# GpSimd adds the attention scores of four column tiles; TensorE sums the denominators from two such sums

## What is computed

```python
h = relu(layernorm(x))
Wh, We = h @ W, entity_embs @ W
scores = (Wh @ a1)[:, None] + (We @ a2)[None, :]
e = where(scores > 0, scores, 0.2 * scores)
e = where(adj > 0, e, -9e15)
attention = softmax(e, axis=1)
x = x + elu(attention @ entity_embs + h)
h = relu(layernorm(x))
x = x + (adj == 1) @ h + h
```

## Time and profile before

| | |
|---|---|
| time, median of three runs | 415.71 us (415.42 to 417.8) |
| the profiled execution's own time | 416.58 us |
| its span in the trace | 414.8 us |
| TensorE, VectorE, ScalarE, GpSimd busy | 87%, 74%, 44%, 27% of the span |
| mean granted clock of TensorE | 0.947 of full |

### The profile page before, as it was taken

The page is one execution under the profiler, slowest core; times in us unless marked ns, Lnnn a source line. Parts: engine busy times, 40 slices in busy tenths (PEclk is TensorE's granted clock), DMA queues, the critical chain, the costliest instruction groups (busy, mean ns, idle before and its releaser), DMA issues. The chain is left out here.

```text
span 414.8 us, 5569 instructions
## 1 busy us (share of the span) xinstructions
PE 360.7 (87%) x2295; PEld 126.6 (31%) x2295; DVE 306.9 (74%) x329; ACT 184.0 (44%) x205; POOL 112.1 (27%) x165
## 2 busy tenths in 40 slices
PE   0679935999976889999978999998899999999996
PEld 0254611221121113233222332332223323334564
DVE  3182068979997998989979789799897899934211
ACT  1130104566644656754356556544565546542100
POOL 5189801111111114125111241101112498000500
PEclk9967765999999699999999999999899999999999
DMA  6999997777869687669885997899999950000011
GB/s 226 236 214 201 212 213 145 132 126 134 147 113 156 90 128 127 120 110 134 151 120 98 141 162 132 89 108 104 88 92 92 107 59 0 2 2 0 2 52 51
DMA packets 15848, 47.85 MB, mean 115 GB/s; under 512 B 1552, under 2 KB 1616, under 8 KB 15568
## 3 DMA queue, kind: packets, MB, share of 16 engines
q0 software_dynamic: 14656, 44.05, 70.1%
q1 hardware_dynamic: 1168, 3.46, 2.2%
HBM read 111.46 MB, written 1.05 MB: 271 GB/s over the span
## 5 line engine op out<-in xcount | busy, mean ns | idle before, releaser
L589 ACT ACTIVATE yp<-yp,tbias 128x1024 f32<-128x1024 f32 x128 | 146.7, 1149 | 118.5 <-DVE yp L806 117.2
L806 DVE SCALAR_TENSOR_TENSOR yp<-s8b,t8neg,am 128x1024 f32<-128x1024 f32 x128 | 162.3, 1288 | 17.5 <-PE pb L1078 16.8
L1065 PE MATMUL pb<-yp,enta 128*64 128x512 f32 x512 | 140.6, 631 | 27.6 <-ACT yp L589 27.3
L722 DVE TENSOR_TENSOR am<-am,vx 128x2048 uint16<-128x2048 uint16 x64 | 79.2, 1237 | 1.8 <-ACT vx L517 1.8
L384 POOL DMA_DIRECT2D am<-adj_t x64 | 35.2, 558 | 163.3 <-DVE yp L806 163.0
L1078 PE MATMUL pb<-yp,onesf 128*32 128x512 f32 x512 | 69.1, 612 | 0.1
L1065 PEld LDWEIGHTS pb<-yp,enta 128*64 128x64 f32 x512 | 28.7, 139 | 103.0 <-ACT yp L589 69.6
L993 PE MATMUL pb<-am,h 128*64 128x512 bf16 (+1 forms) x432 | 55.8, 383 | 0.0
L993 PEld LDWEIGHTS pb<-am,h 128*64 128x64 bf16 x432 | 26.5, 111 | 40.5 <-issue 29.7
L393 POOL DMA_DIRECT2D am<-adj_t x14 | 10.0, 711 | 58.5 <-DVE yp L806 58.5
L1078 PEld LDWEIGHTS pb<-yp,onesf 128*32 128x32 f32 x512 | 10.2, 109 | 39.3 <-issue 36.7
(11 more groups left out here) (145 smaller groups left out, 259.5 us busy)
## 6 DMA issues: line engine op xcount, KB each, us to landing
am<-adj_t POOLq DMA_DIRECT2D x78, 512.0 KB, 7.7
edge<-adj_t POOLq DMA_DIRECT2D x6, 512.0 KB, 9.4
enta<-ent SPq DMA_DIRECT2D x1, 1040.0 KB, 5.2
xs<-xt SPq DMA_DIRECT2D x1, 1024.0 KB, 10.7
out<-yp SPq DMA_DIRECT2D x4, 256.0 KB, 2.0
mats<-eye SPq DMA_DIRECT2D x1, 256.0 KB, 6.2
wt_sb<-w_t SPq DMA_DIRECT2D x1, 32.0 KB, 2.1
a_sb<-a_cols SPq DMA_DIRECT2D x1, 0.5 KB, 2.0
```

Of the source, the lines that this page charges most:

```text
L589: sc.activation(y, y, ACT.Exp, bias=tbias[:, at:at + 1]).then_inc(exp_done, 1)
L722: v.tensor_tensor(at, at, vx[:, b % 2, 0:width(b)].bitcast(U16).unsqueeze(1).to_broadcast([P, tiles(b), width(b)]), ALU.bitwise_xor).then_ ...
L806: v.scalar_tensor_tensor(out=yp[:, n % YS, 0:W], in0=s8b[:, b % 2, 0:W], scalar=t8neg[:, at:at + 1], in1=am[:, (chunk0[b] + c) % RING, jt ...
L1065: t.matmul(acc2(b)[s * D:(s + 1) * D, :], enta[:, tile_at(b, jt), 0:D], yp[:, n % YS, s * HALF:(s + 1) * HALF], start=(jt == 0), stop=(jt ...
```

## The change

GpSimd gets an addition. For each group of four steps it adds their four score buffers into one of two new buffers `ysum` (128 x 1024 float32): nothing at the first step of the group, `yp + yp` at the second, `ysum + yp` at the third and fourth. That is done for the first 120 steps, 90 additions in all, each of which waits for `exp_done`, and the later ones for the sum before (`y_summed`). TensorE makes denominators only at steps that are multiples of 8, from the two sums, four matmuls in place of sixteen. The last eight steps keep the old way. `pv_done` rises with each step's numerators, and VectorE waits for `y_summed` (in the last steps `dens_done`) as well before it overwrites a score buffer. There are five score buffers in place of four, two `edge` buffers in place of four, and four edge loads in place of six go to them; the other 16 go into the ring. The step numbers of `FIN`, `LONE_AT` and the first `PIECE_AT` shift, and the four diagonal additions of `own` are spread over four steps.

```diff
-YS = 4
+YS = 5
+DIRECT_STEPS = 8
...
-PIECE_AT = (47, 51, 57, 61, 67, 71, 79, 83, 88, 92, 96, 100, 104, 108, 112, 116, 120, 124)
+PIECE_AT = (48, 52, 58, 62, 68, 72, 80, 84, 89, 93, 97, 101, 105, 108, 112, 116, 120, 124)
...
-EDGES = 4
-RINGED = 6
-LOAD_AT = (28, 34, 56, 62, 70, 74)
+EDGES = 2
+RINGED = 4
+LOAD_AT = (28, 34, 66, 70)
...
+    POOLED = STEPS_ALL - DIRECT_STEPS
+    def sums_with(n):
+        return n // 8 + 1 if n < POOLED else POOLED // 8 + (n - POOLED) // 2 + 1
...
+            def add_scores(n):
+                a = ysum[:, n // 4 % 2]
+                if n % 4 == 0:
+                    return
+                pool.wait_ge(exp_done, n + 1)
+                if n % 4 == 1:
+                    if n >= 8:
+                        pool.wait_ge(dens_done, n // 8)
+                    g.tensor_tensor(a, yp[:, (n - 1) % YS], yp[:, n % YS], ALU.add).then_inc(y_summed, 2)
+                else:
+                    pool.wait_ge(y_summed, n)
+                    g.tensor_tensor(a, a, yp[:, n % YS], ALU.add).then_inc(y_summed, 1)
...
+                if n < POOLED:
+                    add_scores(n)
...
                     dve.wait_ge(pv_done, n - YS + 1)
+                    if n - YS < POOLED:
+                        dve.wait_ge(y_summed, n - YS + 1)
+                    else:
+                        dve.wait_ge(dens_done, sums_with(n - YS))
...
-                if jt % 2 == 1:
-
-                    if jt == 1 and b >= 1:
-                        pe.wait_ge(den_sb, first[b])
-                    for r in range(2):
-                        for s in range(2):
-                            at = r * D + s * 32
-                            mm = t.matmul(dens[at:at + 32, :], onesf[:, 0:32],
-                                          yp[:, (n - 1 + r) % YS, s * HALF:(s + 1) * HALF],
-                                          start=(jt == 1), stop=(jt == NT - 1), tile_position=(0, at))
-                    mm.then_inc(pv_done, 2)
+                if n % 8 == 0 and 0 < n <= POOLED:
+
+                    b2 = (n - 1) // NT
+                    if n - 8 == b2 * NT and b2 >= 1:
+                        pe.wait_ge(den_sb, first[b2])
+                    pe.wait_ge(y_summed, n)
+                    denominators(ysum[:, 0], ysum[:, 1], n - 8 == b2 * NT, n == (b2 + 1) * NT)
+                if n >= POOLED and n % 2 == 1:
+                    denominators(yp[:, (n - 1) % YS], yp[:, n % YS], False, n == STEPS_ALL - 1)
```

More of the change, by code:

```diff
@@ L121, in graph_layers @@
     VROWS = [t + 1 for t in SHIFTS]
-    FIN = [dict(den=1, inv=2, bc=3, t=4, e=4, c=6, xc=7, sq=7, var=8, vs=9, h=11, hi=11, r=12, mid=12, lo=14)
+    FIN = [dict(den=2, inv=3, bc=4, t=5, e=5, c=7, xc=8, sq=8, var=9, vs=10, h=12, hi=12, r=13, mid=13, lo=15)
            ] * (NB - 1)
-    LONE_AT = 6
+    LONE_AT = 10
+    POOLED = STEPS_ALL - DIRECT_STEPS
+    def sums_with(n):
+        return n // 8 + 1 if n < POOLED else POOLED // 8 + (n - POOLED) // 2 + 1
     ctx = ExitStack()
@@ L143, in graph_layers @@
         yp = sb("yp", [P, YS, 2 * HALF], F32)
+        ysum = sb("ysum", [P, 2, 2 * HALF], F32)
         s8b = sb("s8b", [P, 2, 2 * HALF], F32)
@@ L305, in graph_layers @@
         pv_done = sem("pv_done")
+        y_summed = sem("y_summed")
+        dens_done = sem("dens_done")
         den_sb = sem("den_sb")
@@ L349, in own_at @@
         def own_at(v):
-            return PIECE_AT[v] - 3
+            return PIECE_AT[v] - 6
         block = ctx.enter_context(nc.Block())
@@ L458, in deviations, with own @@
                 g.tensor_tensor(rstd[:], rstd[:], mhalf[:], ALU.pow).then_inc(rstd_ready, 1)
-            def own(w):
+            def own(w, tiles_of):
                 p, j = ORDER[w]
@@ L465, in own @@
                 pool.wait_ge(edges_in[w], 16)
-                for i in range(SUB):
+                for i in tiles_of:
                     e = edges(w)[:, i, at + i * P:at + (i + 1) * P]
                     g.tensor_tensor(e, e, eyeb[:], ALU.add, saturate=False).then_inc(own_ready, 1)
+            def add_scores(n):
[10 more added lines that the diff above has]
+                    g.tensor_tensor(a, a, yp[:, n % YS], ALU.add).then_inc(y_summed, 1)
             def edges_at(u):
@@ L485, in _ @@
                 for w in OWN:
-                    if w < PIECES and n == own_at(w):
-                        own(w)
+                    if w < PIECES and 0 <= n - own_at(w) < SUB:
+                        own(w, (n - own_at(w),))
+                if n < POOLED:
+                    add_scores(n)
             for w in OWN[4:6]:
-                own(w)
+                own(w, range(SUB))
             deviations(NB - 1)
             for w in OWN[6:]:
-                own(w)
+                own(w, range(SUB))
         @block.scalar
@@ L520, in sums_out @@
                 act.wait_ge(pv_done, (b + 1) * NT)
+                act.wait_ge(dens_done, sums_with((b + 1) * NT - 1))
                 if b >= 1:
@@ L968, in variance_again, with denominators @@
                 mm.then_inc(hn_ps, 1)
+            def denominators(y0, y1, start, stop):
+                for r, y in enumerate((y0, y1)):
+                    for s in range(2):
+                        at = r * D + s * 32
+                        mm = t.matmul(dens[at:at + 32, :], onesf[:, 0:32], y[:, s * HALF:(s + 1) * HALF],
+                                      start=start, stop=stop, tile_position=(0, at))
+                mm.then_inc(dens_done, 1)
             def neighbours(v, i):
@@ L1064, in _ @@
                 for s in range(2):
-                    t.matmul(acc2(b)[s * D:(s + 1) * D, :], enta[:, tile_at(b, jt), 0:D],
-                             yp[:, n % YS, s * HALF:(s + 1) * HALF],
-                             start=(jt == 0), stop=(jt == NT - 1), tile_position=(0, s * D))
+                    mm = t.matmul(acc2(b)[s * D:(s + 1) * D, :], enta[:, tile_at(b, jt), 0:D],
+                                  yp[:, n % YS, s * HALF:(s + 1) * HALF],
+                                  start=(jt == 0), stop=(jt == NT - 1), tile_position=(0, s * D))
+                mm.then_inc(pv_done, 1)
                 for v, at in enumerate(PIECE_AT):
```

## The result

The changed kernel takes 577.57 us (median of four runs, 576.4 to 577.68) against 416.1 us in the same rounds: a ratio of 1.387, with an interval of 1.384 to 1.390. The forecast was 564 us, in a range of 505 to 618 us. The profiled execution has a span of 575.8 us, 161.0 us more than before.

The account below looks back on a forecast made before the run. VectorE and TensorE, both about 90% busy in the steps, were taken as the bound. From 416.6 us, +180 for additions, -14 hidden and -19 for TensorE's saved work gave 563.6 us, range 505 to 618 us.

Parts of the forecast that it names:

- The mechanism: In the steps, GpSimd additions reading SBUF exclude VectorE's two-SBUF-input instructions for 1.55 to 2.45 us each; chance 0.78.
- The rival "hidden": GpSimd's reads interleave with VectorE's scores, so only TensorE's saved work counts: 398 us, chance 0.03.
- The fixed price: Each GpSimd addition costs VectorE 0.19 us whatever its length: 415 us, no change, chance 0.03.
- Something between: The port lock is given up within an addition, or VectorE pays half: 481 us, chance 0.06.
- GpSimd as the pace: In the steps, additions wait for the sum before and for VectorE, so GpSimd paces them: 617 us, chance 0.10.
- data time of an addition: Part of a 128 x 1024 GpSimd addition that moves data and holds VectorE: 2.0 us of 2.2 us.
- 90 additions on VectorE, before hiding: In the steps each addition holds VectorE for its data time: 90 x 2.0 = 180 us added.
- hidden in VectorE's idle time and PSUM work: Additions overlapping VectorE's remaining idle time and PSUM-reading instructions in the steps, about half of 28 us: -14 us.
- VectorE's idle time in the steps: VectorE's waits for the denominators' matmuls to free a score buffer all go: 16.8 us saved.
- TensorE's end behind the scores, and the start: TensorE finishes closer behind the last score, where it ended 5.7 us behind before: 2 us saved.
- The steps priced at nothing: GpSimd's queue, added waits over sums, moved loads and shifted pieces cost nothing or nearly so.
- relief: TensorE loses 45 us of denominator work in the steps; with VectorE following at once, worth 19 us: 398 us alone.

Follow-up runs that it names:

- other_data: Changed kernel with the additions reading a constant table and VectorE no longer waiting for them before overwriting a score buffer: 582.55 us, ratio 1.3998.
- write_only: Changed kernel with each GpSimd addition replaced by a constant fill of the same 128 x 1024 buffer, same waits: 400.06 us, ratio 0.9620.
- psum_input: Changed kernel without the second layer, and with the scores reading one input from PSUM instead of SBUF: 463.03 us, ratio 1.1130.
- half_width: Changed kernel with each GpSimd addition working on 512 columns in place of 1024: 481.27 us, ratio 1.1571.
- relief_only: Changed kernel without the additions or VectorE's wait for them; TensorE multiplies constant buffers at every eighth step: 399.73 us, ratio 0.9602.
- uncoupled: Changed kernel with TensorE's denominators reading a constant table, and neither TensorE waiting for the sums nor GpSimd for TensorE: 572.31 us, ratio 1.3756.
- neither: Changed kernel without GpSimd additions, with the old denominators behind every second step, all else kept: 413.57 us, ratio 0.9933.
- adds_only: Changed kernel with its additions kept but the sums unread; TensorE makes the old denominators behind every second step: 572.39 us, ratio 1.3769.
- one_input: Changed kernel with each GpSimd addition replaced by a 128 x 1024 tensor_scalar reading one score buffer: 462.31 us, ratio 1.1121.
- the control: Changed kernel without the second layer, scores still reading SBUF, plus one small tensor_scalar in each block: 549.59 us, ratio 1.3207.

## Why the prediction was right, and where it was off

*The mechanism* stands. That VectorE is held for each addition's data time was read from seven instructions of 128 elements and one of 1024 in the trace of before; `other_data`, `write_only` and `psum_input` take away in turn the dependency, GpSimd's reading and the scores' second SBUF input. With `other_data` the scores are still held (2.01 us), with `write_only` VectorE's whole busy time in the steps is back at 271.0 us, and with `psum_input` the scores are free (1.273 us). The rival "hidden" is out by the scores' 2.10 us. The fixed price is out by `half_width`, which costs half. "Something between" is out by 3.37 - 1.21 = 2.16 us, nearly the whole 2.33 us of an addition alone. GpSimd as the pace is out: in the steps VectorE is busy 443.2 of 460.8 us and sat idle before the scores for an addition 2.3 us in all.

One reading does not bear the reason that the prediction gives beside it. L658, on which "for GpSimd's whole instruction" rests, is a `tensor_scalar` with one SBUF input, and not of the kind with two that the prediction then speaks of. It was held all the same, as L713 is in `psum_input`. For the two-input instructions the trace of before had only L468's short meetings, and the runs supplied the rest.

*The terms.* The span grew by 161.0 us; the steps are read from the stretches.

| | forecast | measured |
|---|---|---|
| data time of an addition | 2.0 us | 2.16 us by the shift, 2.33 us alone |
| 90 additions on VectorE, before hiding | +180 us | 90 x 2.16 = +194.4 us |
| hidden in VectorE's idle time and PSUM work | -14 us | (443.2 - 271.9) - 194.4 = -23.1 us |
| VectorE's idle time in the steps | -16.8 us | (460.8 - 443.2) - 29.3 = -11.7 us |
| TensorE's end behind the scores, and the start | -2 us | +1.4 us |
| sum | +147 us | +161.0 us |

The 2.16 us are read from one shift; the score at 328.27 us gives 3.44 - 1.27 = 2.17 us. The hidden part is what is left of VectorE's growth when 90 times that is taken off, so it carries any error of this price.

The largest error is the price of one addition: L422 understated it (1.90 us against 2.33 us). It differs from an addition in its broadcast operands and in that it multiplies, and no run separates the two; the 0.3 us added for the dense operands, scaled from 65 elements, was too little in any case. The GPSIMD Engine Reference of the Trainium skill (elementwise cycle accounting) gives 4497 ns for 2048 elements, so by halves, as an estimate, 2.25 us for the whole addition; measured alone it is 2.33 us, so that estimate was nearer than my 2.2 us. The hidden part errs by 9 us the other way and makes up for some of it: that the sum came within 14 us is in part this luck.

The next is VectorE's idle time. I let all 16.8 us of waits go. In `relief_only` the idle time in the steps falls from 29.3 to 285.4 - 270.8 = 14.6 us, 14.7 us of the 16.8; in the changed kernel it is 3 us more than that, and 2.5 us of those go in `uncoupled`, with the waits between TensorE and GpSimd over two buffers that I had priced at nothing because VectorE has five. The last is TensorE's end: at 6.9 us (532.2 - 525.3) it is not closer behind the scores than before.

*The steps priced at nothing* hold but for those 2.5 us: `neither` has the moved pieces, loads and buffers, without additions and relief, and is 0.7% faster than the kernel before, and `write_only` has the changed order of GpSimd's queue as well, and takes the relief's time. The relief was forecast at 398 us and is 399.73 us. TensorE's lower clock, kept for the upper end, cost nothing that the runs can show: `adds_only` gives it the 45 us back to do in the steps and the time falls, and `uncoupled` falls as far at the low clock.

## What to carry to other kernels

Work on GpSimd is not free because GpSimd is idle: ask what VectorE's instructions read. If most of them have two inputs in SBUF, as here, each GpSimd instruction that reads SBUF adds most of its own duration to VectorE's time (67 to 85% of it in the table above). Here that cost 178 us (577.6 - 399.7) to save work that was worth 16 us. A short GpSimd instruction in the trace of the old kernel, compared with the same one elsewhere and with its neighbours on VectorE, shows this before anything is built. Two kinds of work got by without waiting here: GpSimd's fills beside VectorE's scores, and scores that read PSUM and one SBUF input beside GpSimd's additions.

## What the runs showed of the hardware

GpSimd's reading with one input also holds VectorE's two-input instructions (`one_input`), while writing alone does not hold them at all (`write_only`), though VectorE writes too. A VectorE instruction that waits pays the rest of the addition whatever its own size: in `psum_input` a 128 x 8 `tensor_tensor` (L714) took 2.04 us in the mean and 2.86 us at most, where that size took 0.17 us before. SBUF — State Buffer of the Trainium skill (the two separate sides) names two kinds of VectorE instruction that GpSimd excludes: one with two SBUF inputs, only against a GpSimd instruction that reads SBUF, and one in a 2-port mode, against any. The runs agree on the first. L658 and L713, with one SBUF input, were held too; whether they belong to the second kind, and whether a fill would hold them, no run shows.

The turn-taking is not always fair. In `other_data` VectorE waits for nobody in its first steps, and the first addition, GpSimd's first and then VectorE's first instruction behind its pause, looks like this:

```profile
67.94 22.03 POOL L491 TENSOR_TENSOR ysum<-enta 128x1024 f32<-128x1024 f32 x1 [17.78 <-ACT yp L618]
```

```profile
107.84 1.42 DVE L837 SCALAR_TENSOR_TENSOR yp<-s8b,t8neg,am 128x1024 f32<-128x1024 f32 x1 [20.07 <-PE pb L1105]
```

The addition stood for 22 us while VectorE's instructions followed one another. VectorE's last one ended at 87.78 us and the addition at 89.97 us, 2.2 us later, so it looks as if nearly all of it was done only then. VectorE then paid with a wait of 20 us, behind TensorE, which waited for the sums. In the changed kernel the first addition took 6.7 us in the same way, and the five buffers stopped VectorE after that; with scores that read PSUM (`psum_input`) it took 3.2 us, and the first fill of `write_only` 0.96 us. Later additions of this size took at most 3.5 us each, but for one of 4.5 us in the control. Why the first one does not get its turn was not tried and stays open.
